# Gated delta attention with a perceptron on one core: where the perceptron's norms, roots, variances and low parts stand in the last seven steps

## What is computed

```python
x = x + layernorm(attention(layernorm(x)))   # 8 sequences of 512 tokens, width 256
x = x + layernorm(perceptron(layernorm(x)))
# attention, for each of 16 heads (keys and values 128 wide):
#   q, k, v = silu(conv4(x @ Wqkv)); q, k scaled to length 1
#   M = M * exp(g_t); M = M + k_t (v_t - k_t M) * beta_t; o_t = q_t M
#   out = rms(o) * norm_w * silu(z); out @ Wout, summed over the heads
# perceptron: relu(x @ W1 + b1), relu(. @ W2 + b2), . @ W3 + b3   (256 -> 512 -> 512 -> 256)
```

## Time and profile before

| | us |
|---|---|
| median of three runs (2730.87 to 2734.3) | 2731.98 |
| profiled execution, its time | 2731.75 |
| profiled execution, span from first to last instruction | 2730.0 |
| PE busy in the span | 2636.8 (97%) |
| ACT busy | 2248.2 (82%) |
| DVE busy | 2244.3 (82%) |
| POOL busy | 2019.0 (74%) |

### The profile page before, as it was taken

How to read it: one execution, slowest core, us unless ns; L and a number is a source line. 1 busy time by engine, 2 the same in 40 slices (tenths; PEclk the granted TensorE clock), 3 DMA queues, 4 the chain that set the end, 5 groups by cost and what they waited for, 6 DMA issues and landing times.

```text
span 2730.0 us, 71108 instructions
## 1 busy us (share of the span) xinstructions
PE 2636.8 (97%) x23972; PEld 2308.8 (85%) x23972; DVE 2244.3 (82%) x4904; ACT 2248.2 (82%) x7476; POOL 2019.0 (74%) x1823
## 2 busy tenths in 40 slices
PE   5899999999999999999999999999999999987998
PEld 4688888888888888888888888888888888876786
DVE  6788888888888888888888888888888888875353
ACT  4688888888888888888888888888888888876675
POOL 3477787787787777787777877877877777765564
PEclk8999999999999999999999999999999999998999
DMA  6222222222222222222221222222222223210010
GB/s 221 84 94 102 73 102 94 81 94 97 77 104 82 84 102 78 97 96 80 93 104 71 104 94 73 102 90 85 96 84 88 104 72 126 95 51 32 21 42 32
DMA packets 77957, 238.82 MB, mean 87 GB/s; under 512 B 8480, under 2 KB 23712, under 8 KB 61472
## 3 DMA queue, kind: packets, MB, share of 16 engines
q1 hardware_dynamic: 77600, 234.26, 24.3%
HBM read 221.12 MB, written 13.11 MB: 86 GB/s over the span
## 4 chain that ended last, share of the span: by engine, by line
PE 90%; DVE 4%; issue 2%; ACT 2%; POOL 1%; DMA 0%; DVEq 0%; SPq 0%; ACTq 0%; POOLq 0%
PE pj L1331 26%; PE pj L1486 9%; PE tr L1338 9%; PE g L1378 8%; PE st L1440 5%; PE op L1460 4%; PE op L1461 4%; PE st L1470 4%; PE st L1447 3%; PE g L1513 2%; PE bk L1399 2%; PE bk L1410 2%; PE bk L1413 2%; PE pj L1513 1%; PE bk L1430 1%
## 5 line engine op out<-in xcount | busy, mean ns | idle before, releaser
L996 DVE SCALAR_TENSOR_TENSOR conv<-pj,cw,conv 128x511 f32<-128x511 f32 (+2 forms) x1152 | 847.5, 745 | 51.2 <-ACT conv L687 37.3
L1331 PE MATMUL pj<-xt,w_hi 128*128 128x512 f32 x2048 | 686.3, 417 | 7.0 <-issue 7.0
L494 POOL TENSOR_TENSOR kq<-kq,cum 128x512 f32<-128x512 f32 x256 | 441.5, 1744 | 0.0
L1331 PE MATMUL pj<-xt,w_lo 128*128 128x512 f32 x1024 | 404.9, 395 | 0.0
L523 POOL TENSOR_TENSOR inv<-inv,x 128x512 f32<-128x512 f32 x128 | 148.1, 1157 | 344.9 <-ACT inv L746 344.9
L1331 PEld LDWEIGHTS pj<-xt,w_hi 128*128 128x128 f32 x2048 | 349.5, 191 | 53.2 <-issue 7.1
L687 ACT ACTIVATE conv<-pj,cw 128x512 f32<-128x512 f32 x384 | 266.1, 693 | 124.7 <-PE pj L1331 114.8
L1073 DVE TENSOR_TENSOR y<-bk,mask 128x256 f16<-128x256 f32 x512 | 216.5, 423 | 176.3 <-PE bk L1399 170.0
L530 POOL TENSOR_TENSOR attn<-attn,part 128x512 f32<-128x512 f32 x256 | 326.8, 1277 | 3.1 <-ACT part L769 3.1
L706 ACT ACTIVATE squares_out<-tr 128x128 bf16<-128x128 f32 x1024 | 273.6, 299 | 46.2 <-PE tr L1338 46.2
L1486 PE MATMUL pj<-wo,yt 128*128 128x256 f32 x1024 | 285.7, 402 | 0.8 <-DVE yt L1126 0.8
(11 more groups left out here) (265 smaller groups left out, 7889.7 us busy)
## 6 DMA issues: line engine op xcount, KB each, us to landing
xt<-xt_scratch SPq DMA_DIRECT2D x126, 1024.0 KB, 4.8
decay<-decay_scratch SPq DMA_DIRECT2D x128, 256.0 KB, 5.3
cum<-cumdecay_scratch SPq DMA_DIRECT2D x128, 256.0 KB, 5.5
w_raw<-in_w_heads SPq DMA_DIRECT2D x16, 512.0 KB, 7.1
xt_scratch<-xt SPq DMA_DIRECT2D x8, 512.0 KB, 4.6
x_in<-in_x SPq DMA_DIRECT2D x8, 512.0 KB, 4.0
out<-kq SPq DMA_DIRECT2D x16, 256.0 KB, 2.3
kq<-in_x SPq DMA_DIRECT2D x6, 512.0 KB, 5.6
```

Source lines behind the costliest of these rows:

```text
L494: last = nc.gpsimd.tensor_tensor(part, part, of(cum, p)[:, :], ALU.mult)
L996: nc.vector.scalar_tensor_tensor(out=conv[:, i, j:SEQ], in0=pj[:, i % 2, 0:SEQ - j], scalar=cw[:, i, p // NSEQ, TAPS - 1 - j:TAPS - j], in ...
L1331: last = nc.tensor.matmul(pj[:, i % 2, :], w[:, kt, cols], x_[:, kt, :], start=(n == 0), stop=(n == 3 * KT - 1))
```

## The change

Four kinds of work change their place. No instruction is added or removed on any engine.

- ScalarE: norm 0 of sequences 0 and 1 (steps -2 and 0) and norm 1 of sequence 0 (step -1) are done a chunk at a time, at four places of the step, where all four chunks stood together. `fill(0, a)` itself moves from ahead of `out_squares`, `high_b`, `state_input(1)` and `take(4)` to behind them, and `fill(3, a)` from ahead of `state_input(2)` and `take(6)` to behind them. With them move norm 0 of sequence 2 and `hidden` of steps 1 to 3.
- GpSimd: `root(1, b)` moves from behind `scale_kq` to the very start of a step (`fill(-1, a)`). `hidden_low(0, 3)` and `hidden_low(1, 3)` move from behind `inverse` to behind the low part before them, ahead of `add(1)` and `inverse`.
- VectorE: the variance of norm 0 moves behind `state(2)`, the sums with `x_in` move behind `residual`, `rhs(3)` and `fill_low`.

```diff
@@ gpsimd, fill
+                if i == -1 and step in (-1, 1, 2):
+                    root(1, (-1, 1, 2).index(step))
                 if i == 0:
-                    if step in (-1, 1, 2):
-                        root(1, (-1, 1, 2).index(step))
...
                     elif 1 <= step <= 3:
                         hidden_low(step - 1, (2, 2, 3)[step - 1])
+                        if step < 3:
+                            hidden_low(step - 1, 3)
                 elif i == 2:
                     if step in (-3, -1, 0):
                         root(0, (-3, -1, 0).index(step))
-                    elif 1 <= step <= 2:
-                        hidden_low(step - 1, 3)
@@ gpsimd, the loop
+                fill(-1, a)
                 scale_b(a - 1)
@@ scalar, normed and fill
-                last.then_inc(norm_done, 1)
+                if CH - 1 in chunks_:
+                    last.then_inc(norm_done, 1)
...
-                if i == 0 and step in (-2, 0, 1):
-                    normed(0, (-2, 0, 1).index(step))
-                if i == 1 and step in (-1, 1, 2):
-                    normed(1, (-1, 1, 2).index(step))
+                if i < CH and step in (-2, 0):
+                    normed(0, (-2, 0).index(step), (i,))
+                if 1 <= i <= CH and step == -1:
+                    normed(1, 0, (i - 1,))
+                if i == 0 and step == 1:
+                    normed(0, 2)
+                if i == 1 and step in (1, 2):
+                    normed(1, step)
@@ scalar, the loop
-                fill(0, a)
                 out_squares(a - 4)
                 high_b(a - 1)
                 state_input(1, a - 3)
                 take(4, a - 2)
+                fill(0, a)
...
                 convolve(K, a)
-                fill(3, a)
                 state_input(2, a - 3)
                 take(6, a - 2)
+                fill(3, a)
@@ vector, the loop
-                fill(1, a)
                 convolve(K, 1, a)
                 convolve(K, 2, a)
                 state(2, a - 3)
+                fill(1, a)
                 convolve(K, 3, a)
-                fill(2, a)
                 residual(a - 2)
-                fill(3, a)
                 rhs(3, a - 3)
                 fill_low(a)
+                fill(2, a)
+                fill(3, a)
```

## The result

| | before | changed |
|---|---|---|
| median of six runs, us | 2731.82 | 2711.56 |
| lowest to highest, us | 2730.87 to 2734.3 | 2707.89 to 2713.15 |
| profiled execution, span, us | 2730.0 | 2711.2 |

The ratio of the times is 0.9923, with a 95% interval of 0.991 to 0.9936.

What follows compares the result with a forecast made beforehand. TensorE was taken as the bound, with 30.6 us idle plus low clock in six late steps. Gains of 9.0 + 0.8 + 0 + 7.5 + 2.4 = 19.7 us off 2731.98 gave 2712.3, stated as 2712.5, range 2707 to 2718.5.

Steps and rivals of the forecast that it cites:

- Part 1: Step -1: GpSimd's earlier root removes TensorE's 7.01 us wait and most low clock behind it; 9.0 us (8 to 9.5).
- Part 2: Steps -3 and -2: output-bank wait of 0.86 us goes, VectorE gains 0.4, rhs(3) costs 0.5; 0.8 us (0 to 1.7).
- Part 3: Step 0: shorter waits for m and yr are offset by sums delaying the next mask; 0 us (-1.5 to +1.5).
- The rival with GpSimd: Step 0: VectorE's sums and scalings held up beside GpSimd's instructions, costing 3.6 us; time 2716, chance 0.12.
- Part 4: Step 1: waits for output bank, state_input(2) and hidden_low(0, 3) go, fifth level is waited for; 7.5 us (4.5 to 10).
- Part 5: Steps 2 and 3: waits of 1.30 and most of 1.03 us go, root lets norm 1 follow; 2.4 us (1 to 3.3).
- The slower case: Steps -3 to 2: TensorE's clock low much longer, slower beyond 19.7 us of such work; 2738 with 26 us, chance 0.02.
- the case in which the wait only moves: Step -1: something else was also late, so the project starts no earlier; about 8 us stay, time 2724, chance 0.06.
- signs of being wrong: Clock below 0.95 in step -1; x or t wait over 4 us; step-0 sums over 1.2 each; step 3 and rest not 184.

Runs made afterwards that it cites:

- e9: Changed kernel with the two sums with x_in of step -2 back around the residual; median 2710.77 us, ratio 0.9922 to the kernel before.
- e12: The changed kernel run again without edit, as a control; median 2714.02 us, ratio 0.9935 to the kernel before.
- e1: Kernel before with only GpSimd's root of norm 1 moved to the front of the step; median 2723.97 us, ratio 0.9967.
- e6: Changed kernel with GpSimd's root of norm 1 behind scale_kq again; median 2719.18 us, ratio 0.996 to the kernel before.
- e10: Changed kernel with the two norms of step 1 moved from ScalarE to VectorE; median 2709.15 us, ratio 0.9914 to the kernel before.
- e2: Kernel before with only ScalarE's edit (norms in chunks, fills later); median 2724.36 us, ratio 0.9972.
- e5: Changed kernel with VectorE's order of before; median 2712.12 us, ratio 0.9933 to the kernel before.
- e4: Kernel before with only VectorE's moves; median 2731.75 us, ratio 0.9995.
- e3: Kernel before with only hidden_low(0, 3) and hidden_low(1, 3) ahead of GpSimd's add and inverse; median 2726.61 us, ratio 0.9982.
- e8: Changed kernel with norm 0's statistics (sequences 0 and 1, steps -3 and -1) in the step's first half; median 2711.81 us, ratio 0.993 to the kernel before.
- e11: Changed kernel with the edits of e8, e9 and e10 together; median 2704.52 us, ratio 0.9898 to the kernel before.

## Why the prediction was right, point by point

The sum was 19.7 us and the time 20.3. That they agree to 0.6 us is in part luck: the six steps gave 17.9 us in one execution and 20.2 in the other, the clock alone moves step 1 by 2.6, and the parts miss on both sides, by -2.6, +0.8, +1.3, -0.8 and -0.5 us. By steps it was this (the one column is the forecast by parts, the other the steps that belong to it):

| part | forecast | measured |
|---|---|---|
| 1, step -1 | 9.0 (8 to 9.5) | 6.4; 8.7 with the sums back (e9) |
| 2, steps -3 and -2 | 0.8 (0 to 1.7) | 1.6 |
| 3, step 0 | 0 (-1.5 to 1.5) | 1.3 |
| 4, step 1 | 7.5 (4.5 to 10) | 6.7; 9.3 in e12 |
| 5, steps 2 and 3 | 2.4 (1 to 3.3) | 1.9 (step 2) |

**Part 1: right in mechanism, and mis-sized.** The root runs ahead of the scaling of b, the 7.01 us go as a whole, and e1 and e6 price the root at 7.7 and 7.6 us. What failed is that nothing was charged to the pairs at the start of the step: "does not shorten VectorE's own queue" is true, but the sums behind `rhs(3)` make it longer, since the wait for TensorE's state that they used to cover is now open (0.52 us before r). That is 0.93 us of wait, and the clock fell on top of it, which cost 1.3 (e9, e10); the last 0.35 of the missing 2.6 is the part's own. The statement that a clock below 0.95 in step -1 would show me wrong was tested by the trace: it was 0.93.

**Part 2: right in its net, not in its terms.** The gain of 1.63 us in the two steps less the 0.93 that came back in the next is 0.70, against 0.8. I had charged 0.5 for `rhs(3)` and put it in these two steps; it stands in step -1. Of the 1.63, 0.87 are ScalarE's (e2: 21.08 to 20.21) and the rest is VectorE's (0.45 and 0.30 by e5; 0.45 and 0.56 in e4), where the forecast had 0.4 for it.

**Part 3: inside its bounds, but not zero.** ScalarE's share went as argued: the 0.86 us for the output bank went, and the waits for the fifth level and the one behind it grew from 0.78 and 0.39 to 1.38 and 0.88. TensorE in step 0 of the changed kernel:

```profile
2473.20 0.29 PE L1405 MATMUL bk<-t,b_hi 128*128 128x64 f16 x4 [1.38 <-ACT t L740]
...
2476.01 0.29 PE L1405 MATMUL g<-t,b_hi 128*128 128x64 f16 x4 [0.88 <-ACT t L740]
...
2478.99 0.49 PE L1453 MATMUL st<-m,kq 128*128 128x128 f32 x2 [0.44 <-DVE m L1098]
...
2481.44 0.40 PE L1436 MATMUL bk<-x,yr 128*128 128x128 f16 x4 [1.97 <-DVE yr L1088]
```

The waits for m and yr fell in sum from 3.52 to 2.41 us, by 1.1 where 1.2 was forecast; of that 0.67 came with ScalarE's edit alone (e2: 1.24 and 1.61). What failed is the last step of the part, that the sums behind the low parts would give this back by holding up the next step's mask. They did not: between 2486.45 and the fifth level at 2499.22 TensorE waits nowhere over 0.3 us in the changed kernel, and step 0 gained 0.95 us from VectorE's moves alone (e4) and lost 1.04 when they were taken back (e5). Step 1 says nothing clear on it: with the moves it is 1.53 us longer in e4 (the wait for last_h and the clock, above) and 0.83 shorter than in e5.

**The rival with GpSimd.** VectorE's sums in steps 0 and 1 of the changed kernel; those of step -2, with GpSimd idle up to 2436.84, took 1.28 us for the two (above). Then the two scalings of step 0 in the kernel before.

```profile
2482.76 2.09 DVE L1163 TENSOR_TENSOR attn<-attn,x_in 128x512 f32<-128x512 f32 x2
...
2507.94 3.21 DVE L1163 TENSOR_TENSOR attn<-attn,x_in 128x512 f32<-128x512 f32 x2
```

```profile
2484.57 1.13 DVE L1141 TENSOR_SCALAR shift<-mmv 128x4 f32<-128x4 f32 x1
2485.62 1.30 DVE L1142 TENSOR_SCALAR ve<-mmv 128x4 f32<-128x4 f32 x1
```

So the sums are held up by 0.8 and 1.9 us beside GpSimd's work. The rule of the Trainium skill that the prediction weighed (SBUF — State Buffer, Who interferes with whom) agrees with this. The rival fails on the price and on the place: it counted 3.6 us in step 0, and there 0.8 fell on sums that nothing of the pairs waits for and 0.5 on one scaling (0.67 us against 0.17). It overlooked that the kernel before was held up more: its two scalings took 1.13 and 1.30 us and the first sum 1.57, which is 3.0 us over the 0.17, 0.16 and 0.67 of the free ones, against 1.3 in the changed kernel. So in step 0 VectorE is held up less in the new order than before. Step 1 in e4 shows the rival at work where TensorE does wait, on last_h.

**Part 4: right, near its middle.** The 3.14, 1.75 and 2.29 us went, a wait of 3.00 on ScalarE's fifth level came (3 to 3.5 forecast), and the clock fell behind it. I had taken 2.0 us off for the clock; in the two executions of the same code the fall behind this wait is worth 1.58, and with the stretch from step 0 it is 2.56. Where the clock stayed up (e12), the part's sum without that deduction, 9.5 us, meets 9.3, and the second layer starts 17.77 us into the step against 24.45 before, 6.7 us earlier where 6.9 was forecast. The low part in front of `inverse` was forecast at 2.29 + 2.6 = 4.9 us and brings 5.1 by itself (e3); ScalarE's moves bring 3.25 (e2). All but VectorE's edit gives 5.9 (e5), less than the two together, but by no more than the clock moves this step, so that the two get in each other's way is not shown.

**Part 5: 0.5 us too much.** ScalarE's edit alone gives 2.01 us in step 2 (e2), the root none (e1, 21.03). The two waits of 1.30 and 1.03 us, 2.33 in sum, went, and the step became 1.87 shorter; the wait of 0.51 us for r stayed. That the root lets norm 1 of sequence 2 follow at once, which the part's upper end priced at 1 us, brought nothing.

**The slower case** needed 19.7 us more of work at the low clock. TensorE had less of it, not more: the clock column rose in all three long steps, and the waits of 1.24 us and less left it at 1.00 in steps -3 and -2. One number of the case in which the wait only moves does not follow: parts 2, 4 and 5 are 10.7 us, not 8, which makes 2721.3.

**What stays open.** Two of the prediction's signs of being wrong came true beside a time that was right: the clock of 0.93 in step -1, and a rest of 182.2 us behind step 2 in place of 184. Which of the waits of 2 to 3 us brings the clock down, and why the same wait does in one execution and not in another, was seen and not explained. Neither was the stretch of 182.2 to 184.4 us after step 2, which differs in executions of the same code.

## What to carry to other kernels

The place of an instruction of 1 us in a queue was worth 7 to 8 us here (e1, e6): its input was there 11 us before its turn came, and the queue had a gap at that time. Look at when the input is there, not at how long the instruction takes. Work moved behind a wait that it used to cover opens that wait; count it (0.93 us here), and look for a stretch of another engine's queue where the same work covers idle time (e8 to e10 together gave 6.5 to 8.8 us more in that way, e11). When waits of several us are removed, give the low clock behind them a price of its own, for it was half of the gain in step 1 of e3, and let the range hold it both ways. And run the same kernel twice: what one step gained by the clock alone (2.6 us) is as much as several of the edits here.
